# One loop of steps for recurrence, routing and shared expert in a two-layer gated block on one core

## The reference, cut to what matters

```python
# recurrence; k = layernorm(x), v = ctx_2048, w = -exp(time_decay), u = time_first
y_t = (e1 * aa + e2 * vt) / (e1 * bb + e2)
aa, bb = e1b * aa + e2b * vt, e1b * bb + e2b
x = x + tanh(g_xattn[0]) * y
# experts; flat = layernorm(x)
logits = flat @ router_w
scores = softmax(logits); _, topk_idx = top_k(logits + router_bias, 4)
comb = scores of the four, divided by their sum
routed = einsum('ne,nef,efd->nd', comb, silu(flat @ wg) * (flat @ wu), wd)
shared = einsum('nsh,shd->nd', silu(flat @ swg) * (flat @ swu), swd)
x = x + tanh(g_ffn[0]) * (routed + shared)
# then cross attention on ctx_2048 (keys with an RMS norm), and a second
# feed-forward whose weights and activations are rounded to fp8 by blocks of 32
```

## Time and profile before

| what | us |
|---|---|
| median of 3 runs (lowest to highest) | 545.86 (544.14 to 548.65) |
| profiled execution: its own time | 542.03 |
| profiled execution: span, first to last instruction | 540.3 |
| mean granted TensorE clock | 0.87 |
| busy: PE, DVE, ACT, POOL | 405.7, 355.9, 163.3, 239.5 |

### The profile page before, as it was taken

The page is one execution under the profiler, slowest core; times in us unless marked ns, Lnnn a source line. Parts: engine busy times, 40 slices in busy tenths (PEclk is TensorE's granted clock), DMA queues, the critical chain, the costliest instruction groups (busy, mean ns, idle before and its releaser), DMA issues.

```text
span 540.3 us, 8236 instructions
## 1 busy us (share of the span) xinstructions
PE 405.7 (75%) x2711; PEld 273.3 (51%) x2711; DVE 355.9 (66%) x896; ACT 163.3 (30%) x390; POOL 239.5 (44%) x336
## 2 busy tenths in 40 slices
PE   0677653469779399999889776488886599999884
PEld 0466432224347266567667454366664255555553
DVE  1748889995362105559786725477853599999992
ACT  1445421113200144445334450335353122222210
POOL 2445543413300766766661246756210345555441
PEclk9998875559959589999899975589999699999998
DMA  6116999910025945666786562224200000000000
GB/s 198 52 59 195 281 301 220 222 48 1 1 49 108 323 122 164 176 182 177 164 166 145 161 195 59 78 83 145 67 24 2 1 0 12 10 10 11 10 10 19
DMA packets 72088, 57.38 MB, mean 106 GB/s; under 512 B 38896, under 2 KB 64624, under 8 KB 72048
## 3 DMA queue, kind: packets, MB, share of 16 engines
q1 hardware_dynamic: 61808, 38.28, 27.0%
q0 software_dynamic: 4608, 12.59, 10.4%
q10 hardware_dynamic: 5632, 6.00, 3.4%
HBM read 42.18 MB, written 14.68 MB: 105 GB/s over the span
## 4 chain that ended last, share of the span: by engine, by line
PE 35%; issue 24%; DVE 21%; POOL 9%; ACT 4%; DMA 4%; SPq 1%; POOLq 0%; DVEq 0%; ACTq 0%
PE psum L1153 8%; PE psum L1247 6%; PE psum L1294 4%; PE psum L1285 3%; POOL arena_dn L610 3%; PE psum L1308 3%; POOL mx_w L613 2%; DVE arena_dn L860 2%; PE psum L1367 2%; PE psum L1311 2%; DMA ys_dram<-ysb 2%; DMA x_res<-in_x_dram 2%; PE psum L1424 2%; PE psum L1432 1%; PE psum L1453 1%
## 5 line engine op out<-in xcount | busy, mean ns | idle before, releaser
L536 POOL DMA_INDIRECT shared<-h_dram,tok_u x64 | 64.0, 1000 | 57.8 <-PE psum L1270 28.6
L1453 PE MATMUL psum<-arena_dn 128*128 128x512 f32 x128 | 59.0, 615 | 3.7 <-ACT arena_dn L794 3.7
L1153 PE MATMUL psum<-ident,arena_dn 128*128 128x128 f32 x112 | 22.9, 331 | 51.5 <-DVE arena_dn L839 15.9
L1153 PEld LDWEIGHTS psum<-ident,arena_dn 128*128 128x128 f32 x112 | 15.1, 166 | 58.1 <-issue 24.0
L1033 DVE TENSOR_TENSOR h1T<-psum,h1T 128x128 f32<-128x128 f32 x32 | 9.3, 291 | 49.6 <-ACT h1T L716 37.2
L1453 PEld LDWEIGHTS psum<-arena_dn 128*128 128x128 f32 x128 | 24.4, 196 | 33.7 <-issue 27.9
L610 POOL TENSOR_TENSOR arena_dn<-arena_dn 128x512 f32<-128x512 f32 x16 | 20.3, 1272 | 44.9 <-DVE arena_dn L1004 44.9
L560 POOL DMA_INDIRECT arena_up<-ys_dram,slot_u x32 | 31.3, 977 | 11.3 <-issue 11.0
L1153 PE MATMUL psum<-ident,arena_up 128*128 128x128 f32 x128 | 23.0, 303 | 15.5 <-DVE arena_up L1056 5.0
L1153 PE MATMUL psum<-ident,mx_w 128*128 128x128 f32 x128 | 24.4, 333 | 12.5 <-POOL mx_w L613 9.6
L1247 PE MATMUL psum<-h1T,shared 128*128 128x512 f32 x64 | 30.9, 644 | 0.0
(11 more groups left out here) (216 smaller groups left out, 995.2 us busy)
## 6 DMA issues: line engine op xcount, KB each, us to landing
ys_dram<-ysb SPq DMA_DIRECT2D x32, 256.0 KB
arena_up<-in_L_ffn_wg_dram SPq DMA_DIRECT2D x8, 512.0 KB, 8.0
arena_up<-in_L_ffn_wu_dram SPq DMA_DIRECT2D x8, 512.0 KB, 7.9
arena_dn<-in_L_ffn_wd_dram SPq DMA_DIRECT2D x4, 1024.0 KB, 11.4
h1T<-in_L_ffn_wd_dram SPq DMA_DIRECT2D x64, 64.0 KB
va_dram<-mx_w ACTq DMA_DIRECT2D x8, 256.0 KB, 3.9
kT_dram<-mx_w ACTq DMA_DIRECT2D x8, 256.0 KB, 4.8
arena_up<-kT_dram SPq DMA_DIRECT2D x8, 256.0 KB
```

The lines of the kernel that those rows point to most:

```text
L536: pool.indirect_dma_start(out=xg[n % 4][:, b, :], out_offset=None, in_=h1_dram[:, :], in_offset=bass.IndirectOffsetOnAxis(ap=tok_u[:, 2 * ...
L1153: return pe.transpose(dst, src, ident[0:k, 0:k])
L1453: ins = pe.matmul(bank[2 + 2 * part + h][:, :], xTF[s][:, c, :], mx_gu[:, c, lo:lo + HW], start=(c == 0), stop=(c == C - 1))
```

## The change

Recurrence, routing and the up half of the shared expert become one loop of 12 steps on every engine. In step k, DVE does `xnA` of tile k, the residual and layer norm statistics of tile k-3, one scan of tile k-1, `h1B` of k-3, the division of k-2, the top four of k-3, the ranks of k-4. The shared expert is cut into 16 chunks of 256 columns, two in each of steps 5 to 12, and its down half into eight tiles, of which four are in steps 7 to 10. The four scans become one of 516 elements. Banks 0 and 6 are now used by every tile, not in turn. `mask` is made by two sums on POOL instead of one reduction on DVE. The weights of the four are made once for all tiles, behind `tok`. In the table DVE makes `poh` and POOL makes `boh`. `h1B` has four buffers, is stored directly, and the copies into `h1S` and `h1T` are gone. SP's order is new, and so is `weight_halves`.

```diff
 def weight_halves(n):
-    return min(min(max(n - 4, 0), NPS - 5) + 9 * max(n - NPS + 1, 0) // 4, 2 * NWC)
+    return min(max(min(n, NPS - 1), 0) + 2 * max(n - NPS + 1, 0), 2 * NWC)
+def shared_chunks(k):
+    return [4 * ((k - 5) // 2) + 2 * ((k - 5) % 2) + x for x in range(2)] if 5 <= k < 5 + T else []
...
# SP, behind x, the context tiles and the shared weights (unchanged)
+            up_load(range(0, 48, 16), "moe_in")
+            for n in range(4):
+                h1_store(n)
+            down_load(range(0, E // 2, 16), "moe_in")
+            sp.wait_ge(sem("wT_ps"), 8)
+            (loads of gate_v and up_v into mx_w, 1 MB each, moved here)
+            for n in range(4, T):
+                h1_store(n)
+            sp.wait_ge(sem("combs"), 1)
+            sp.wait_ge(sem("tok"), 1)
+            down_load(range(E // 2, E, 16), "moe_in2")
+            for b in range(4):
+                sp.wait_ge(sem(f"h1_out{b}"), 16 * (T // 4))
+            sp.wait_ge(sem("hs"), 2 * T)
+            up_load((48,), "moe_in3")
+            sp.wait_ge(sem("sdown"), T)
+            sp.dma_start(mx_w[:, 4096:6144]..., down_v).then_inc(sem("mx_in2"), 16)
# POOL
+            for n in range(T + 5):
+                s, i, m = n % 2, n - 2, n - 3
                 (pu of tile n)
+                if 0 <= i < T:
+                    inv_sqrt(rstd[:, i % 2:i % 2 + 1], mv[:, i % 2, 1:2], LN_EPS, "mvB", i + 1, "rstdB")
+                if 1 <= n <= T:
+                    key_rms(n - 1)
                 (den, num of tile n; pairs, mask, macc of tile m)
+                for x in shared_chunks(n):
+                    pool.tensor_tensor(hs[q % 2][:, f, :], sgt[x % 2], upt[x % 2], ALU.mult).then_inc(sem("hs"), 1)
+            pool.wait_ge(sem("slot_u"), 2)
+            for n in range(T * K):
+                reach(pool, sem("tab_ps"), n - 3)
+                pool.tensor_scalar(boh[n % 4], iota[:, 0:NG], blkf[:, n:n + 1], tokid[:, n // K:n // K + 1],
+                                   ALU.is_equal, ALU.mult).then_inc(sem("blocks"), 1)
# ACT
+            for k in range(T + 5):
                 (pexp of k-4)
+                n = k - 2
+                    act.wait_ge(sem("rk"), n + 1)
+                    act.activation(knS[:, :, 0:HD], bank[6][:, 0:D]..., ACT.Copy, scale=rk[:, n:n + 1])
                 (exponentials and vTs of k; squares and vaS of k-1; h1T of k-3; kTS of k-2 and its stores; shared chunks)
# DVE
+            for k in range(T + 4):
                 (xnA of k)
+                n = k - 3
+                    dve.wait_ge(sem("yT_ps"), n + 1)
+                    dve.scalar_tensor_tensor(x_res[:, n, :], bank[4][:, 0:D], ...).then_inc(sem("x1"), 1)
+                    (bn_stats, bn_aggr).then_inc(sem("mvB"), 1)
+                n = k - 1
+                    chain(dve.tensor_tensor(ekp[s][:, 1, :, 1:P + 1], ekp[s][:, 0, :, 1:P + 1], vTs[n % 3], ALU.mult), "r")
+                    dve.tensor_tensor_scan(sums[s]..., decays..., ekp[s]..., 0.0, ALU.mult, ALU.add)
+                n = k - 3
+                    dve.wait_ge(sem("rstdB"), n + 1)
+                    if n >= 4:
+                        dve.wait_ge(sem(f"h1_out{n % 4}"), 16)
+                    dve.tensor_scalar(h1B[n % 4], x_res[:, n, :], ...).then_inc(sem("h1"), 1)
                 (division of k-2)
+                n = k - 3
+                    dve.wait_ge(sem("logits"), n + 1)
                     (maximum, biased, top four, one-hot rows)
+                n = k - 4
+                    dve.wait_ge(sem("rank"), n + 1)
                     (prod2 and its reduction)
+                if 0 <= k - 7 < 4:
+                    shared_sum(k - 7)
...                 (slot numbers; table with poh alone; tok)
+            (shared_sum of tiles 4 to 7, the two memsets, then for all tiles at once:)
+            chain(dve.tensor_tensor(tmp..., onehot, pexp..., ALU.mult), "r")
+            chain(dve.tensor_reduce(ck..., tmp, AX.X, ALU.add), "r")
+            (sum, reciprocal, two small products).then_inc(sem("combs"), 1)
# PE
+            for k in range(T + 4):
                 (kvT of k: waits for exps and vTs of k-1, since bank 0 is shared)
+                n = k - 1
+                    reach(pe, sem("knS"), n)
+                    reach(pe, sem("vaS"), n)
                     (kv_ps of k-1 into bank 6)
                 (transpose of knS of k-2)
+                if 0 <= k - 7 < 4:
+                    shared_down(k - 7)
+                for x in chunks[:1]:
+                    shared_up(x)
                 (h1T and logits of k-3; rank of k-4)
+                for x in chunks[1:]:
+                    shared_up(x)
                 (yT of k-2)
+            for n in range(T * K):
+                table(n)
+                if n == 7:
+                    shared_down(6)
+                if n == 15:
+                    shared_down(7)
-            pe.wait_ge(sem("moe_in"), 16 * 18)
-            pe.wait_ge(sem("moe_in2"), 16 * 2)
+            pe.wait_ge(sem("moe_in"), 16 * 14)
```

More of the change, by code:

```diff
@@ L126, in build_program @@
         h1T = sb("h1T", [P, C, N])
+        xgT1 = sb("xgT1", [P, 1024])
+        ysb = [sb(f"ysb{i}", [P, 2, D]) for i in range(2)]
         shared = sb("shared", [P, 3072])
@@ L227, in build_program @@
         i8 = take(8, dt=U32)
-        ck = take(K)
-        cs = take(1)
-        rcs = take(1)
-        prod = take(K, E)
-        prod2 = take(K, E)
+        pairs = take(2, E, dt=BF16)
+        mask = [take(E, dt=BF16) for _ in range(2)]
+        take = carver(arena_up[:, 14336:16384])
+        h1B = [take(D) for _ in range(4)]
+        sgt = [take(2 * P) for _ in range(2)]
+        upt = [take(2 * P) for _ in range(2)]
+        take = carver(arena_dn, E * D // 2)
+        ck = take(T, K)
+        cs = take(T)
+        rcs = take(T)
         cnt_i = take(E, dt=I32)
@@ L262, in build_program @@
         dnS = [take(2, D) for _ in range(2)]
-        ysb = [sb(f"ysb{i}", [P, 2, D]) for i in range(2)]
         def own(tile):
@@ L333, in experts_of @@
             return values
+        sd_ps = [bank[b][:, D:2 * D] for b in (4, 4, 4, 4, 4, 0, 6, 1)]
         block = ctx.enter_context(nc.Block())
@@ L1253, in _ @@
-            pe.wait_ge(sem("rc"), T)
-            def table_pe(at):
-                i = at(0)
-                if i is None:
-                    return
-                pe.wait_ge(sem("onehots"), i.n + 1)
-                first = isinstance(i.n, int) and i.n == 0
-                last = isinstance(i.n, int) and i.n == T * K - 1
-                pe.matmul(bank[5][:, 0:NG], poh[i.slot], boh[i.slot], start=first, stop=last)\
-                    .then_inc(sem("tab_ps"), 1)
-            run_steps(pe, T * K, 0, 4, table_pe, lead=T)
@@ new lines, in _, with table @@
+            pe.matmul(bank[5][0:1, P:2 * P], eidm, ident[:, :], start=True, stop=True).then_inc(sem("eid_ps"), 1)
+            for x in shared_chunks(T + 4):
+                shared_up(x)
+            pe.wait_ge(sem("kTS"), T)
+            pe.wait_ge(sem("vaS"), T)
+            pe.wait_ge(sem("xs"), 4)
+            for t in range(4, 6):
+                shared_down(t)
+            def table(n):
+                pe.wait_ge(sem("onehots"), n + 1)
+                pe.wait_ge(sem("blocks"), n + 1)
+                pe.matmul(bank[2][:, 0:NG], poh[n % 4], boh[n % 4], start=(n == 0), stop=(n == T * K - 1))\
+                    .then_inc(sem("tab_ps"), 1)
```

502 lines of the change are left out of this document (230 added, 272 removed).

## The result

The changed kernel takes 590.57 us (median of 4 runs, 587.63 to 594.73) beside 545.0 us for the kernel before: ratio 1.085, 95% interval 1.080 to 1.090. I had forecast 541 in a range of 522 to 557, so sign and range were wrong. Ratios are of the fast executions of a kernel and times in us medians of all of them, and the traces of a1_keyfirst and b1_splate are of slow ones (573.58 and 578.38 us, where their fast ones have medians of 563.8 and 571.4). The profiled execution took 592.06 us, where the sum in the prediction gives 537.3 for a profiled one: 54.8 us to be found.

What follows compares the result with a forecast made beforehand. The front was taken as a line of DVE-bound, then PE-bound stages, replaced by one cycle. The experts' 14.8 us lead shrinks to 3.0, PE's run-ahead adds 1.7: 4.7 us faster, 541 in place of 545.86, range 522 to 557.

Steps and rivals of the forecast that it cites:

- The cycle with PE's wait for `knS`: Merged loop: one dependence from `x1` through all engines sets each step, with PE's `kv` waiting for `knS`.
- slot numbers to the table's first factor: Behind the loop: slot numbers on DVE take the same 9.3 us as before, 142.8 to 152.1.
- `tok` to `combs`: Start of the experts: sums, memsets, product and reduction put `combs` 9.2 us behind `tok`, at 174.9.
- ACT's wait for a `ys` store: Start of the experts: third `ysb` copy waits some 10 us for the first store, until 199; undisturbed 187.2.
- The first `x1`: Start of tile 0's residual sum, the loop's first, forecast at 36.4 us.
- The step: Length of one loop step: 9.8 us for step 3, 10.6 for 4, 12.4 for 5 and 6, 14.5 for 7 and 8.
- The third rival: Loop with PE at 1.2 GHz: 27.6 us more if always, 14 if half the time, so 555; chance 0.24.
- the one scan instead of four: DVE in the loop: saves up to 1 us, costs up to 1, counted as nothing beside PE's part.
- 12.6 us wait for `h1_out`: Loop, tile 4: DVE waits for tile 0's `h1` store behind the weight loads; that step costs 6.6 us more.
- For a pair I took 0.40: Token table split between DVE and POOL: 0.33 to 0.53 us a pair, 0.40 taken, 12.8 us in all.
- the lock rival: Table: DVE and GpSimd exclude each other, 0.53 us a pair, total 4 us more, 545; chance 0.06.
- The first `ys` store lands 21.1 after `combs`, and 3 more: SP's queue: 3 MB, four up loads of 2.62 us and the store take 21.1, gathers 3 more, until 199.

Runs made afterwards that it cites:

- a1_keyfirst: Changed kernel with GpSimd taking the key's inverse square root ahead of that of `x1`'s statistics in each step: 568.6 us, ratio 1.050 to the kernel before.
- b1_splate: Changed kernel with the late loads (experts 48 to 63, `down_w`) issued one by one between the `ys` stores: 572.6 us, ratio 1.052 to the kernel before.
- a3: Changed kernel with 24 unused identity transposes on PE ahead of the wait for `knS` in steps 3 to 8: 572.1 us, ratio 1.064 to the kernel before.
- b0_after: The changed kernel unedited, measured again as the yardstick: 584.8 us, ratio 1.075 to the kernel before.
- a2_noload: Changed kernel with the shared expert's Silu replaced by a Copy, so no table loads in the loop: 572.2 us, ratio 1.066 to the kernel before.
- b3_all: Changed kernel: key's root first, shared weights early, silu by Tanh, table factors on VectorE, down products behind table, late loads between `ys` stores: 544.1 us, ratio 1.000.
- d1_best: b3_all plus stores of `h1` tiles 0 to 3 between expert loads, and GpSimd's products `hs` ahead of its masks: 531.2 us, ratio 0.988 to the kernel before.

## Why the prediction was wrong

What held is the mechanism of the loop. The cycle with PE's wait for `knS`, slot numbers to the table's first factor (9.3 us, measured 9.1), `tok` to `combs` (9.2 us, measured 9.1), and ACT's wait for a `ys` store are in the trace as forecast. The first `x1` (36.4, measured 36.24) is a hit with some luck, since it lies between 32.8 and 36.7 in the thirteen traces; and the size of ACT's wait (11.8 by my sum, measured 11.2) is all luck, as both of its ends came 10 us late. Four terms failed.

**The step.** I took `kv` as "47.35 to 49.68 is 2.33" from a stage in which PE had a clock of 0.91, and carried it into a cycle whose design makes PE idle just ahead of it. It measured 4.4 us. The third rival priced the low clock, at 27.6 us "if always", and I gave it 0.24 against the evidence I had written beside it: that steps 3 and 4 are like the routing stage with 0.52. "With the chunks PE is busy 60% and more from step 5" was true (66 and 62%) and did not keep the clock up (0.67 and 0.81).

**What a moved operation meets.** ACT's Silu and Exp had been in different stages, and the kernel before loads two tables in its whole front. In one loop they alternate: 13 loads of 1.28 us. I listed every instruction of the step and forgot the one that the order of functions creates. The Trainium skill (ScalarE: Activation LUTs, section What ACT_TABLE_LOAD costs) gives a switch about 2.66 us, of which 1.28 are the load and the rest a drain. Here the load is 1.28 and the next activation starts 0.02 us behind it, so the trace has half of that price.

**The one scan.** I wrote that "the one scan instead of four" counts nothing, since it lies beside PE's part of the cycle. It lies beside POOL's root too, which is in the cycle, and adds 0.9 us to it.

Each alone, in `x1` spread against the first trace's 122.9: clock 10.7 us with what a3 could restore, tables 9.6, scan 7.0, together 27; against b0_after's 121.5 it is 9.3, 8.3 and 5.6, together 23. Missing before the slot numbers were 27.7. They were measured one at a time and on different chips, so that the sum comes near is support and no proof. There is one more item: the 12.6 us wait for `h1_out`, 6.6 of them in the sum, did not occur, because the step was already late by more. It appeared when the loop became quicker, 2.8 us in a1_keyfirst, 4.3 in a2_noload and 11.2 in b3_all. So the spread was in fact 33 us longer than mine without it (32 in b0_after), and 6 to 9 us of that are in none of the three edits; the shared chunks and the down product at the lower clock (3.4 us for the chunk from 79.69 to 83.08, 2.0 for the one from 93.51 to 95.54) are the likeliest place, and not shown.

**Table and queue.** For a pair I took 0.40 between ends of 0.33 and 0.53, and it was 0.56. That is near the lock rival's value, but not by its mechanism: my 0.33 for a factor came from another kind of operation (a sum of 64 columns in bf16), and GpSimd's comparison with two scalars takes 0.58 by itself. With the 3 us stalls that is the 9.3. "The first `ys` store lands 21.1 after `combs`, and 3 more" was 34.0 (211.80 to 245.77): the four up loads were issued over 21.6 us, not 10.5. b1_splate shows that this queue was worth 12 us. The third copy without the wait would also have been late, 31.9 us behind `tok` (245.77 less 11.22) where I had 21.5, with PE's 4.1 us for gathered rows and a granted clock of 0.58 from its first transposes on, where the kernel before had 0.72; in b1_splate, where the wait is gone, it comes 30.7 behind `tok`.

Of the last 8.0 us, 1.7 are a run-ahead of PE that I had credited. The others are of this one execution: from the third `ysb` copy to the end it took 346.3 us, but b0_after, the same kernel, took 339.8, and the kernel before 340.0. In the first trace the twelve copies behind the third take 42.2 us at a clock of 0.86, in b0_after 39.0 at 0.93, before 38.5 at 1.00; why isn't shown.

Two slips of 0.3 us in the sum cancel: step 8 is listed at 14.5 and added as 14.2, and 152.1, 12.8 and 0.5 make 165.4, not 165.7.

Last, the reach of the range. I had a slower rival on the clock and one on the table, and let the range end at 557, which neither of them reaches with both true: 27.6 and 4 above 541 is 573. The terms were not alternatives, and I had treated them so.

## What to carry to other kernels

- Before stages are merged into one loop, write down the cycle through all engines, and then look at the order *within* each engine for an operation of this step that stands ahead of one that the next engine waits for. Here two tiny instructions on GpSimd, moved ahead of two others, gave 13 to 19 us alone and 22 to 27 with the other edits, and with all of d1_best's edits the merged loop beat the kernel it was made from by 1.2%, in the one measurement there is.
- A duration from a stage in which an engine was busy doesn't hold in a cycle in which it waits. Price such a link at the lower clock unless the profile has one like it that follows a wait.
- When work from two stages shares an engine, look at what depends on the neighbour: the table of the activation function, the other engine's long instructions on the shared port, and which loads stand in front of a short store.

## What the runs showed of the hardware that I had not expected

- Useless work made two steps shorter: 24 transposes a step brought their clock from 0.74 and 0.62 to 1.00 and the steps from 13.3 and 14.3 down to 10.9 and 11.7 us.
- Four scans of 129 elements end 0.15 us later than one of 516 and hold GpSimd's root for 0.67 us in place of 1.48.
- The issue of a 512 KB load takes 0.47 us on SP when loads stand apart, and up to 11.9 when they are issued in a row; the store issued right behind a lone load takes 1.5 to 2.6 us in place of 0.4.
- GpSimd takes 0.57 to 0.58 us for a comparison with two scalars on 64 columns with nothing of VectorE beside it, VectorE 0.30 for the same.
